# A cross-attention and top-1 expert kernel: when the exponentials' units, the first half's maxima, the later queries and the output path take their turns

## What is computed

```python
qh = (layernorm(x) @ Wq.T + bq)            # (2, 1024, 16 heads, 16)
kh = (ctx @ Wk.T + bk); vh = (ctx @ Wv.T + bv)
scores = einsum('blhe,bshe->bhls', qh, kh) * tau + delta
a = softmax(scores / 4, axis=-1)           # over the 154 context tokens
x = x + einsum('bhls,bshd->blhd', a, vh).reshape(B, L, D) @ Wo.T + bo
n = layernorm(x)
top1 = argmax(softmax(n @ router_w + router_b))
x = x + (h_a * sigmoid(h_g)) @ w2[top1] + b2[top1]   # h_a, h_g = split(n @ w1[top1] + b1[top1])
```

## Time and profile before

| | us |
|---|---|
| median of 3 runs | 422.3 |
| lowest and highest | 420.49, 424.15 |
| profiled execution, its own time | 424.38 |
| its span | 422.6 |

### The profile page before, as it was taken

One profiled execution on the slowest core, in us unless ns is written; L12 is line 12 of the kernel. 1 busy time (PEld: TensorE's weight loads), 2 busy tenths in 40 slices (PEclk: granted clock), 3 DMA queues, 4 the chain that ended last, 5 costly groups with the idle time before them and its releaser, 6 DMA issues.

```text
span 422.6 us, 8458 instructions
## 1 busy us (share of the span) xinstructions
PE 385.6 (91%) x2820; PEld 276.1 (65%) x2825; DVE 268.8 (64%) x678; ACT 227.5 (54%) x360; POOL 107.5 (25%) x150
## 2 busy tenths in 40 slices
PE   6969899798999798886999999999999999999991
PEld 2645444455556354754976979788797887978870
DVE  4786885677477763884675666566665666656661
ACT  2315468466365556214857756566465664656640
POOL 4091290011011001107897600000000000143432
PEclk9969799999699999989999999999999999999997
DMA  6676392261011383325987604910049100011211
GB/s 214 163 198 133 76 245 116 64 142 52 4 48 53 98 330 108 120 106 154 338 253 243 198 26 143 414 68 26 26 146 420 55 25 25 8 66 50 74 50 38
DMA packets 26165, 54.05 MB, mean 128 GB/s; under 512 B 6726, under 2 KB 16778, under 8 KB 25994
## 3 DMA queue, kind: packets, MB, share of 16 engines
q1 hardware_dynamic: 20954, 41.48, 30.7%
q0 software_dynamic: 3664, 11.19, 7.9%
q10 hardware_dynamic: 1516, 0.99, 1.1%
HBM read 39.20 MB, written 7.01 MB: 109 GB/s over the span
## 4 chain that ended last, share of the span: by engine, by line
PE 75%; DVE 9%; ACT 4%; issue 4%; DMA 3%; SPq 1%; ACTq 1%; POOL 1%; DVEq 0%; POOLq 0%
PE bank L1169 27%; PE bank L1214 13%; PE bank L1193 5%; PE bank L952 4%; PE bank L962 4%; PE bank L1037 3%; PE bank L901 3%; PE bank L1221 3%; PE bank L864 3%; PE bank L940 2%; PE bank L1012 2%; DVE row_max L1564 2%; ACT probs L1321 2%; DMA delta_sb<-in_delta_dram 1%; PE bank L1064 1%
## 5 line engine op out<-in xcount | busy, mean ns | idle before, releaser
L1169 PEld LDWEIGHTS bank<-slot_io,w_now 128*128 128x128 f32 x1024 | 122.4, 192 | 8.2 <-issue 5.5
L1169 PE MATMUL bank<-slot_io,w_now 128*128 128x128 f32 x1024 | 126.2, 276 | 1.3 <-ACT w_now L1401 0.8
L1828 DVE TENSOR_TENSOR hidden<-bank,b_sb 128x512 f32<-128x512 f32 x64 | 44.2, 691 | 55.9 <-PE bank L1169 55.7
L1401 ACT ACTIVATE w_now<-w_sb 128x1024 f32 x66 | 68.9, 1046 | 10.5 <-issue 10.3
L1414 ACT ACTIVATE gate<-hidden 128x256 f32<-128x256 f32 x76 | 31.6, 415 | 72.5 <-DVE hidden L1828 59.8
L1214 PE MATMUL bank<-w_sb,act_ut 128*128 x256 | 66.9, 384 | 0.0
L1564 DVE TENSOR_REDUCE row_max<-bank 128x3 f32<-128x462 f32 (+1 forms) x96 | 53.2, 579 | 21.1 <-PE bank L901 20.8
L1321 ACT ACTIVATE probs<-bank 128x512 f32<-128x512 f32 x80 | 46.1, 598 | 28.2 <-PE bank L940 19.2
L1214 PEld LDWEIGHTS bank<-w_sb,act_ut 128*128 128x128 f32 x256 | 43.7, 191 | 11.6 <-issue 8.3
L791 POOL DMA_INDIRECT b_lane<-q_parts,lane_row x12 | 11.4, 953 | 111.3 <-DVE hidden L1832 110.1
L901 PE MATMUL bank<-k_stack,q_stack 99*128 99x154 bf16 x256 | 34.5, 247 | 5.3 <-DMA q_stack<-q_split 3.6
(11 more groups left out here) (187 smaller groups left out, 515.2 us busy)
## 6 DMA issues: line engine op xcount, KB each, us to landing
w_sb<-in_weights_dram SPq DMA_DIRECT2D x32, 768.0 KB, 7.0
q_stack<-q_split SPq DMA_DIRECT2D x18, 256.0 KB, 5.2
rows<-row_buf SPq DMA_DIRECT2D x17, 256.0 KB, 2.0
x_sb<-in_x_dram SPq DMA_DIRECT2D x4, 512.0 KB, 5.2
b_sb<-in_b_dram SPq DMA_DIRECT2D x1, 1024.0 KB, 6.2
k_stack<-k_split SPq DMA_DIRECT2D x12, 77.0 KB
q_stack<-q_split ACTq DMA_DIRECT2D x6, 128.0 KB, 3.4
q_stack<-q_split SPq DMA_DIRECT2D x6, 128.0 KB, 4.2
```

The costliest lines, as they stand in the source:

```text
L1169: ins = pe.matmul(h_ps[ring(j)][:, P * m:P * (m + 1)], w1_now[:, ring(j), k, P * m:P * (m + 1)], slot_io[:, tile, P * k:P * (k + 1)], star ...
L1401: act.activation(w1_now[:, ring(j), :, :].rearrange("p k n -> p (k n)"), w_sb[:, bass.ds(buffer + experts[number], 1), 0:KD * 2 * HQ].rear ...
L1828: dve.tensor_tensor(hidden[:, ring(j), :, :], h_ps[ring(j)][:, :].rearrange("p (m n) -> p m n", n=P), b1_now.to_broadcast([P, HIDDEN_BLOCK ...
```

## The change

`UNIT_AT` goes from 3 to -6, and `unit_due` now gives a group of five units six steps: five with a unit, one free. Unit 0 of a chunk is nine steps sooner, groups 1, 2 and 3 start eight, seven and six steps sooner. Half 0's maxima are turned at step 14, not 20. The output path starts at absolute step 24c + 18 (`OUT_AT`), six steps sooner. Chunk 2's queries are three and chunk 3's six steps sooner, chunk 3's layernorm five and six. Chunk 0's scores have four banks for twelve steps only, then two, since the units need the other two. The waits that keep the order in `work_ps[1]` are moved with it: half 1's `turn_max` now comes after `turn_on` of the chunk's first output tile, and `turn_on` of the second comes one step after that `turn_max`.

```diff
--- before.py
+++ after.py
@@ -79,16 +79,18 @@
 EARLY_EXPERTS = 2
 
 
-MAX_AT = ((-1, 20), (0, 1))
-UNIT_AT = 3
+MAX_AT = ((-1, 14), (0, 1))
+UNIT_AT = -6
+OUT_AT = 18
 OUT_PERIOD = 4
+FOUR_BANKS = 12
 TURN_O, NORMALISE, TURN_ON, COPY_ON, PROJECT, RESIDUAL, NORM2, TURN_X2, COPY_X2, ROUTE, LOGITS = 2, 3, 4, 5, 5, 6, 8, 10, 11, 12, 13
 
-STATS1_AT = {3: (0, 2)}
-NORM1_AT = {3: (0, 6)}
+STATS1_AT = {3: (-1, 21)}
+NORM1_AT = {3: (0, 0)}
 BO_AT = (0, 7)
 RANK_CONSTANTS_AT = (0, 10)
-Q_AT = {1: (-1, 2), 2: (-1, 11), 3: (0, 9)}
+Q_AT = {1: (-1, 2), 2: (-1, 8), 3: (0, 3)}
 TURN_X, PROJECT_0, PROJECT_1, LESS_HIGH_0, LESS_HIGH_1, LESS_MID_0, LESS_MID_1 = 0, 2, 4, 5, 6, 8, 9
 HALF = HEADS // KD
 PAIRS = len(Q_PARTS)
@@ -504,17 +506,18 @@
 
         def due(c, i, step):
 
-            chunk, n = divmod(STEPS * (c - 1) + i - step, STEPS)
+            chunk, n = divmod(STEPS * c + i - OUT_AT - step, STEPS)
             return [TPC * chunk + n // OUT_PERIOD] if 0 <= chunk < CHUNKS - 1 and n in range(0, TPC * OUT_PERIOD, OUT_PERIOD) else []
 
         def score_bank(c, i):
 
-            return (score_ps + st_ps)[i % 4] if c == 0 else score_ps[i % 2]
+            return (score_ps + st_ps)[i % 4] if c == 0 and i < FOUR_BANKS else score_ps[i % 2]
 
         def unit_due(c, i, lag):
 
-            chunk, unit = divmod(STEPS * c + i - UNIT_AT - lag, STEPS)
-            return [(chunk, unit)] if 0 <= chunk < CHUNKS and unit < UNITS else []
+            chunk, at = divmod(STEPS * c + i - UNIT_AT - lag, STEPS)
+            group, unit = divmod(at, STEPS // GROUPS)
+            return [(chunk, UNITS_PER_GROUP * group + unit)] if 0 <= chunk < CHUNKS and unit < UNITS_PER_GROUP else []
 
         def q_due(c, i, step):
 
@@ -891,9 +894,9 @@
 
                 if n == 2:
                     pe.wait_ge(v_copied, BATCH)
-                if c == 0 and n >= 4:
+                if 4 <= n < FOUR_BANKS + 2:
                     pe.wait_ge(max_done, n - 3)
-                if c > 0:
+                if n >= FOUR_BANKS + 2:
                     pe.wait_ge(max_done, n - 1)
                 t, m, first, heads = score_step(i)
                 for n in range(heads):
@@ -913,8 +916,8 @@
                 if m == 0 and phase >= 1:
                     pe.wait_ge(on_copied, TPC * phase)
                     pe.wait_ge(x2t_copied, TPC * phase - 1)
-                if m == 1 and phase >= 2:
-                    pe.wait_ge(x2t_copied, TPC * (phase - 1))
+                if m == 1 and phase >= 1:
+                    pe.wait_ge(on_copied, TPC * (phase - 1) + 1)
                 turned = work_ps[1][0:3 * HALF, 0:CHUNK // 2].bitcast(BF16)
                 for t in range(TPC):
                     ins = pe.transpose(turned[:, P * t:P * (t + 1)],
@@ -1022,7 +1025,10 @@
                     pe.wait_ge(x2t_copied, t)
                 elif t % TPC >= 2 and t < TILES - TPC:
                     pe.wait_ge(x2t_copied, t - 1)
-                pe.wait_ge(mt_copied, min(KD * (t // TPC + 2), KD * CHUNKS))
+                if t % TPC == 0:
+                    pe.wait_ge(mt_copied, min(KD * (t // TPC + 1) + 1, KD * CHUNKS))
+                else:
+                    pe.wait_ge(mt_copied, min(KD * (t // TPC + 2), KD * CHUNKS))
                 for k in range(KD):
                     ins = pe.transpose(out_ps(t)[1][:, P * k:P * (k + 1)], attn[:, t % TPC, P * k:P * (k + 1)], ident)
                 ins.then_inc(on_turned, 1)
```

## The result

The changed kernel takes 432.8 us (median of 4 runs, 431.45 to 435.74), the kernel before 422.25 beside it: ratio 1.0237, 95% interval 1.0178 to 1.0296. It is slower by some 10 us, where 419.8 and "the same" were forecast. The profiled execution's own time is 435.74, the highest of the four.

A forecast was written before the change was run, and what follows sets the result against it. PE, busy 91% of the span, was taken as close to the bound in passes 0 to 2. Start and pass 0 +4.2, passes 1 and 2 -1.2, pass 3 -5.5: -2.5 from 422.3 gives 419.8 us, range 415.0 to 424.0.

The forecast's parts named there:

- 16 x 1.3 ... 23.1 instead of 28.6: Pass 3: 16 steps of 1.3 us plus the end from last unit to `turn_o`; 23.1 us instead of 28.6, -5.5.
- +6.4: End of pass -1: step (0, 0) at 52.3 instead of 45.85, +6.4 us (ends +4.5 and +9).
- the 2.43 us of one load: Pass -1, chunk 0's maxima load: 2.43 us from issue to landing, within 3.6 us from turn to landing.
- The high end I gave for the wait: Pass -1, step 18: first unit waits 1.6 us for the load of maxima, ends 0 and 3.
- the low clock that I had put into a rival: Start, in (b): the wait at step 18 lets the clock fall and (0, 0) comes 8 us late.
- the sign I had named myself: Start of pass 1: the forecast is wrong if the shift at (1, 0) is under 2 or over 7 us.
- -2.2: Pass 0: -2.0 for the low clock, -1.2 for statistics, +1.0 net for tile 0's output path; -2.2 us.
- -0.6 each: Passes 1 and 2: -0.3 wait, -0.8 light steps, +0.5 `turn_on`; -0.6 us per pass, -1.2 for two.
- net 0: Passes 1 and 2: free steps add 0.1 to 0.5 us four times, against waits of the same kind now; net 0.
- (c): Rival, every pass: the maxima become the bound and the kernel slower, about +6 over the forecast; 426 us, chance 0.10.
- (b): Rival, passes -1 to 2: shift paid in full, passes 1 and 2 give nothing; +0.5, 423 us, chance 0.13.
- (a): Rival, pass borders: smoothing is worth more, PE stays busy and no clock falls; -6.4, 416 us, chance 0.24.

The follow-up runs named there:

- both repairs: Changed kernel with routing tasks two steps sooner in pass 3 and units in 20 steps without a free one: 1.0025 of before, 1.0083 on another chip.

## Why the prediction was wrong

**Pass 3, the step that failed first.** "16 x 1.3 ... 23.1 instead of 28.6" took a step's mean time and multiplied it by fewer steps. The measured pass is 30.7 us. I read `due` for the output path and moved it, but never asked what else in the list stands at steps of its own. `route_due` does, and its tasks went from just behind `normalise` to just ahead of it: 4.0 us of waits, and the edit that moves them brings 3.2 us at equal clock (30.25 to 27.0 at the list's end) and took a fall of the clock worth some 2 us with it in the first pair (32.3 to 27.0). Even repaired, the end is 3.3 us shorter than before with free steps (30.3 to 27.0), and without them 3.5 where the clock held and 1.4 where it fell, not 5.5. What keeps the rest was not tried apart; I put it down to the output path: a step without scores is not a quantum of time, since the output path of chunk 2 must run down there as well.

**The start.** "+6.4" at (0, 0) was +7.9, which is near; the parts were not. The turn was 2.2 us sooner than I took it and the landing later, because I carried the 2.43 us of one load to another moment; it was 4.3. The 2.43 us were read with the DMA engines already free; the sooner issue fell among the query loads, and the landing came 2.3 us after those had ended. By the Trainium skill ("DMA: Bandwidth & Descriptors", the anatomy of one DMA, there for one issued by GpSimd) a transfer has about 2.0 us of fixed cost; the rows here go from 2.4 to 6.5 us for the same 24 KB, so for a load among others neither figure is a forecast. The high end I gave for the wait, 3 us, is what came (3.11), and with it the low clock that I had put into a rival. By the sign I had named myself, a shift at (1, 0) of over 7 us (it was 8.8), this half of the sum was wrong too.

**Pass 0.** "-2.2" was +0.9. The low clock did leave the pass, as I had it (0.98 granted instead of 0.89; it went into pass -1), and yet the pass grew: at full clock on both sides it is 3.1 us longer. What it took over (units beside its first scores, the first tile's output path) I had at +1.0 net, less 1.2 for the statistics. No run separates these.

**Passes 1 and 2.** "-0.6 each" was +0.7 and -0.4 on the trace, but this hides that the kernel before had a low clock in both: clean against clean it is 30.06 to 31.56, +1.5. Of this the free steps are 1.2. I had called them "net 0" by balancing waits against waits. The idle time of TensorE is indeed alike (2.5 us in pass 1 against 2.4 before); the time from a unit's matmul to TensorE's next one, summed over the 32 of the pass, is 7.6 us instead of 6.7, and 6.8 without free steps. That is 0.9 of the 1.5 us.

**The rivals.** (c), the slower one, gave 426 and was to come from maxima as the bound in every pass. They were not, apart from `turn_on` behind the copy of half 1's maxima, where TensorE waits 0.24 and then 0.80 us for the copy behind it:

```profile
120.86 0.41 PE L1033 MATMUL bank<-consts,attn 128*128 128x128 f32 x2 [0.24 <-ACT max_t L1313]
...
122.48 1.13 PE L1043 MATMUL bank<-wo_sb,attn_nt 128*128 128x256 f32 x4 [0.80 <-ACT attn_nt L1340]
```

The sign of (c) was right by another mechanism. (b), paid in full, was the nearest in kind: the shift is worth nothing even when its accidents are mended. (a), smoothing keeps the clock up at the borders, was half right: passes 1 and 2 have a clock of 1.00 in all eleven traces with the shifted order, where the kernel before has 0.97 and 0.92, though three of its variants kept 1.00 as well. But the changed kernel's start and its pass 3 have the low clock instead, so the time was not won.

**What stays open.** That the query loads hold up the first load is shown by timing alone. Why pass -1 costs 3.5 us after both repairs, and pass 0 3.1 us at full clock, is open: the parts (units, denser queries, the output path) were not told apart with the units present.

## What to carry to other kernels

Before moving one path in a schedule written out by steps, list everything with a step of its own, and check for each engine what now stands in front of what; a task that was harmless just behind an urgent one can cost its full length just ahead of it. A step is not a unit of time: work taken off a stretch that has slack beside it returns little, while work put into a stretch bound by another engine or by a load's landing is paid for. And a transfer's time from issue to landing holds only for the moment at which it was read: look at what the DMA engines carry when the moved issue will fall.

## What the runs showed that I had not expected

The same kernel on the same chip: of the 23 values of the kernel before in one series, the fastest took 418.26 us, the slowest 426.71. In another series of it the run with the highest mean granted clock, 0.987, took 419.5 us, and those at 0.959 took 425.1 to 425.8. What goes with TensorE's clock moves this kernel by 1.4%, more than either repair, and a comparison of two single profiles can show a gain or a loss that neither kernel has.

Beside a long stretch of GpSimd's additions, some of VectorE's small operations run at a third of their speed: 0.66 us for a subtraction on 128 x 32 values that takes 0.19 elsewhere. In the kernel without free steps:

```profile
47.15 11.17 POOL L702 TENSOR_TENSOR x_sb<-x_sb,bo_sb 128x256 f32<-128x256 f32 x16
...
48.63 0.66 DVE L1487 TENSOR_TENSOR max_rest<-row_max,max_split 128x32 f32<-128x32 f32 x1
```

It is so in every trace, the kernel before's too: the subtraction fell among the additions six times in the 17 traces and took 0.66 us each time, and 0.19 us in all 130 other places. VectorE's reductions of the scores took the same inside (0.63 us for three heads) as outside. No run moved the additions away, so it is a firm coincidence and not an experiment.
